# ScalarE makes the negative half of the first attention's features, one set of moments serves two norms, three projections go together, and the last loop's rows are fetched sooner

## What is computed

```python
h = tok(x, W); h = concat([cls, h])
h = h + attn0(layernorm(h))                # elu(q)+1, elu(k)+1, KV = sum K V over the images, @ Wo.T + bo
h = h + ffn0(layernorm(h))                 # see below
h = h + attn1(layernorm(h))                # causal linear attention, 16 heads
h = h + ffn1(layernorm(h))                 # shared SwiGLU + top-1 of 32 routed SwiGLU experts

def attn0(x):  Q = elu(x @ Wq.T + bq) + 1; K = elu(x @ Wk.T + bk) + 1; V = x @ Wv.T + bv; ...
def ffn0(x):
    xn = (x - mean(x)) * rsqrt(var(x) + 1e-5) * ln_scale + ln_bias
    x_attn = xn @ attn_w.T + attn_b + x
    eo = gelu(x_attn @ w1[e] + b1[e]) @ w2[e] + b2[e]      # expert e is fixed by the position
    return gelu(eo @ next_w.T + next_b)
def layernorm(x): return (x - mean(x)) / sqrt(var(x) + 1e-5)
```

## Time and profile before

| what | us |
|---|---|
| three runs of the kernel | 339.25, 343.43, 345.67 (median 343.43) |
| the profiled execution, its own time | 341.32 |
| its span, first to last instruction | 339.5 |
| tokens, 0 to 34.3 | 34.3, PE busy 24.4 |
| first attention, 34.3 to 65.3 | 31.0, PE busy 27.8 |
| start of ffn0, 65.3 to 88.8 | 23.5, PE busy 16.3 |
| rest of ffn0, 88.8 to 177.7 | 88.9, PE busy 86.5 |
| second attention and routing, 177.7 to 247.5 | 69.8, PE busy 62.6 |
| shared expert and first routed turns, 247.5 to 282.2 | 34.7, PE busy 33.1 |
| further turns, 282.2 to 316.9 | 34.7, PE busy 32.8, DMA share 0.90 |
| last turns and the loop, 316.9 to 339.5 | 22.6, PE busy 15.7 |

### The profile page before, as it was taken

How to read it: one execution, slowest core, us unless ns; L and a number is a source line. 1 busy time by engine, 2 the same in 40 slices (tenths; PEclk the granted TensorE clock), 3 DMA queues, 4 the chain that set the end, 5 groups by cost and what they waited for, 6 DMA issues and landing times.

```text
span 339.5 us, 6676 instructions
## 1 busy us (share of the span) xinstructions
PE 299.2 (88%) x2487; PEld 214.7 (63%) x2487; DVE 206.7 (61%) x595; ACT 138.0 (41%) x312; POOL 52.3 (15%) x72
## 2 busy tenths in 40 slices
PE   1997979758989999999999988989799899997965
PEld 1775547648889999999898666765355334552331
DVE  0355494323546557556557899865964899636726
ACT  1012231522332332323264666527334986515641
POOL 0111000011011001011000001010542001111842
PEclk9999797958999999999999999799999999997979
DMA  7999995000633724000000000399955838999541
GB/s 289 392 443 423 419 302 149 2 0 1 247 102 149 248 52 197 2 0 2 2 1 3 2 2 2 109 431 422 429 205 163 356 113 318 342 386 386 82 65 16
DMA packets 12762, 61.57 MB, mean 181 GB/s; under 512 B 1546, under 2 KB 7514, under 8 KB 9146
## 3 DMA queue, kind: packets, MB, share of 16 engines
q1 hardware_dynamic: 10746, 58.25, 45.1%
q0 software_dynamic: 1984, 2.89, 4.3%
HBM read 55.09 MB, written 6.04 MB: 180 GB/s over the span
## 4 chain that ended last, share of the span: by engine, by line
PE 64%; DVE 15%; DMA 12%; issue 4%; ACT 2%; POOL 1%; SPq 0%; DVEq 0%; ACTq 0%; POOLq 0%
PE P L359 16%; DMA arena<-experts_dram 10%; PE P L467 9%; PE P L479 9%; PE P L669 5%; PE P L611 4%; PE P L393 4%; PE P L523 4%; PE P L682 3%; PE P L455 2%; PE P L554 2%; DMA arena<-patches_dram 2%; DVE arena L1046 1%; DVE st L967 1%; DVE arena L1138 1%
## 5 line engine op out<-in xcount | busy, mean ns | idle before, releaser
L359 PE MATMUL P<-arena 128*104 128x256 f32 x288 | 73.8, 397 | 9.1 <-DMA arena<-patches_dram 6.9
L359 PEld LDWEIGHTS P<-arena 128*104 128x104 f32 x288 | 47.5, 177 | 22.3 <-issue 8.1
L1382 POOL TENSOR_TENSOR rstd<-var,mhalf 104x1 f32<-104x1 f32 x40 | 22.0, 550 | 206.1 <-DVE var L969 206.1
L669 PE MATMUL P<-arena,cols 128*32 128x512 f32 x288 | 34.7, 621 | 4.1 <-ACT cols L901 2.8
L876 ACT ACTIVATE arena<-arena 128x1024 f32 x31 | 31.6, 1051 | 14.2 <-SPq L338 8.6
L479 PE MATMUL P<-arena 128*128 128x104 f32 x256 | 29.9, 275 | 2.4 <-ACT arena L804 2.4
L479 PEld LDWEIGHTS P<-arena 128*128 128x128 f32 x256 | 29.7, 192 | 3.1 <-issue 1.4
L467 PEld LDWEIGHTS P<-arena 128*128 128x128 f32 x256 | 30.8, 197 | 1.3 <-issue 0.7
L467 PE MATMUL P<-arena 128*128 128x104 f32 x256 | 30.6, 279 | 0.5 <-issue 0.5
L804 ACT ACTIVATE arena<-P,arena 128x104 f32<-128x104 f32 x64 | 17.0, 348 | 28.7 <-PE P L467 28.7
L611 PE MATMUL P<-cols,arena 128*128 128x416 f32 x64 | 23.8, 520 | 1.8 <-DVE arena L1199 1.8
(11 more groups left out here) (209 smaller groups left out, 485.9 us busy)
## 6 DMA issues: line engine op xcount, KB each, us to landing
arena<-experts_dram SPq DMA_DIRECT2D x18, 1536.0 KB, 9.4
...
arena<-w_dram SPq DMA_DIRECT2D x1, 1024.0 KB, 10.2
...
```

What stands on the lines that cost most here:

```text
L359: last = mm(P[b][0:a.shape[1], col:col + D], a, rhs(c), start=(c == 0), stop=(c == chunks - 1))
L669: last = mm(P[b][part, :], xT[:, c, part], weights(u)[:, c * INNER:(c + 1) * INNER], start=(c == 0), stop=(c == DC - 1), tile_position=(0, ...
L1382: nc.gpsimd.tensor_tensor(rstd[:, :], var[:, :], mhalf[:, :], ALU.pow).then_inc(s["rstd_ready"], 1)
```

## The change

The edits make four pieces.

1. Features. ACT now reads the bank first: `Relu(-(x + b))` into `eA` (the negated bias is made once on DVE in `own`), then `Exp(-eA)`. DVE waits for ACT's read (`z0_sum`), makes max(x + b, 0) into `zA` in one instruction, and adds `eA`. The value tile 0 is read by DVE (`v0_evac(0)`) ahead of the last feature's addition.
2. Norms. `h1_norms` makes one set of moments of `h`. A second column of `var` holds var * (1 + eps) + eps^2; `power` works on both columns, and both normalised rows come from `h`. bo is added to all of `h` beforehand by one POOL instruction over 104 x 2048, behind the eighth norm; so DVE adds the projection straight into `h`.
3. Projections. `wo(0)`, `wo(1)` and `wo(2)` go to banks 0, 7 and 6 and stand ahead of the ffn0 steps; only wo(3) and later stay in them. `wo_read` is gone; `h0_ready` counts in its place.
4. The nop that gives `l_aim_ready` its first count stands in the first fixed turn, behind `aim_static()`.

```diff
+            for g in range(3):
+                wo(g)
             pe.wait_ge(s["wx_in"], 16)
...
-            lagged(GROUPS + 3, [(tr1, 1), (tr2, 3), (nx, 2), (xa, 1), (wo, 0), (up, 1), (but_last(qk1), 3), (but_last(v1), 3), (down, 1)])
+            lagged(GROUPS + 3, [(tr1, 1), (tr2, 3), (nx, 2), (xa, 1), (later_wo, 0), (up, 1), (but_last(qk1), 3), (but_last(v1), 3), (down, 1)])
...
             for n in range(8):
-                act.wait_ge(s["z0_ready"], n + 1)
-                A(eA[:, n % 2, :], eA[:, n % 2, :], ACT.Exp).then_inc(s["exp0_done"], 1)
+                w, m = n // 4, (n // 2) % 2
+                act.wait_ge(s["qk0_done"], n + 1)
+                if n >= 2:
+                    act.wait_ge(s["qk0_ready"], n - 1)
+                A(eA[:, n % 2, :], bank(n % 4, HALF), ACT.Relu, scale=-1.0, bias=own[:, 2 * w + m:2 * w + m + 1]).then_inc(s["z0_sum"], 1)
+                act.wait_ge(s["z0_sum"], n + 1)
+                A(eA[:, n % 2, :], eA[:, n % 2, :], ACT.Exp, scale=-1.0).then_inc(s["exp0_done"], 1)
...
+            V.tensor_scalar(own[:, 0:4], bcol_s[:, BQ0:BQ0 + 4], -1.0, None, ALU.mult).then_inc(s["zeroed"], 1)
...
-                    dve.wait_ge(s["qk0_done"], n + 1)
-                    if n >= 2:
-                        dve.wait_ge(s["qk0_ready"], n - 1)
-                    V.tensor_scalar(zA[:, n % 2, :], bank(n % 4, HALF), bcol_s[:, b:b + 1], None, ALU.add).then_inc(s["z0_sum"], 1)
                     dve.wait_ge(s["z0_sum"], n + 1)
-                    V.tensor_scalar_min(eA[:, n % 2, :], zA[:, n % 2, :], 0.0).then_inc(s["z0_ready"], 1)
+                    V.tensor_scalar(zA[:, n % 2, :], bank(n % 4, HALF), bcol_s[:, b:b + 1], 0.0, ALU.add, ALU.max).then_inc(s["z0_ready"], 1)
                 if n == 0:
                     continue
                 n -= 1
...
+                if n == 7:
+                    dve.wait_ge(s["brow_in"], 32)
+                    v0_evac(0)
                 dve.wait_ge(s["exp0_done"], n + 1)
-                V.scalar_tensor_tensor((qT, kT)[w][:, m, half * HALF:(half + 1) * HALF], zA[:, n % 2, :], 0.0, eA[:, n % 2, :],
-                                       ALU.max, ALU.add).then_inc(s["qk0_ready"], 1)
+                dve.wait_ge(s["z0_ready"], n + 1)
+                V.tensor_tensor((qT, kT)[w][:, m, half * HALF:(half + 1) * HALF], zA[:, n % 2, :], eA[:, n % 2, :], ALU.add)\
+                    .then_inc(s["qk0_ready"], 1)
...
             def h1_norms(g):
                 dve.wait_ge(s["wo_done"], g + 1)
-                V.tensor_tensor(xr2[:, g % 2, :], P[0][0:GT, 0:D], brow_s[0:GT, BO0, :], ALU.add).then_inc(s["wo_read"], 1)
-                dve.wait_ge(s["wo_read"], g + 1)
-                V.tensor_tensor(h[:, g, :], h[:, g, :], xr2[:, g % 2, :], ALU.add).then_inc(s["h0_ready"], 1)
+                if g == 0:
+                    dve.wait_ge(s["bo0_added"], 1)
+                V.tensor_tensor(h[:, g, :], h[:, g, :], P[wo_bank(g)][0:GT, 0:D], ALU.add).then_inc(s["h0_ready"], 1)
                 dve.wait_ge(s["h0_ready"], GROUPS + g + 1)
-                norm(h[:, g, :], xr[:, g % 2, :], "n_ready")
-                dve.wait_ge(s["n_ready"], GROUPS + 2 * g + 1)
-                norm(xr[:, g % 2, :], xr2[:, g % 2, :], "n_ready")
+                link(V.bn_stats(st[:, :], h[:, g, :]))
+                link(V.bn_aggr(mv[:, :], st[:, :]))
+                V.tensor_scalar(var[:, 1:2], mv[:, 1:2], 1.0 + EPS, EPS * EPS, ALU.mult, ALU.add)
+                V.tensor_scalar_add(var[:, 0:1], mv[:, 1:2], EPS).then_inc(s["var_ready"], 1)
+                norms[0] += 1
+                dve.wait_ge(s["rstd_ready"], norms[0])
+                V.tensor_scalar(xr2[:, g % 2, :], h[:, g, :], mv[:, 0:1], rstd[:, 1:2], ALU.subtract, ALU.mult).then_inc(s["n_ready"], 1)
+                V.tensor_scalar(xr[:, g % 2, :], h[:, g, :], mv[:, 0:1], rstd[:, 0:1], ALU.subtract, ALU.mult).then_inc(s["n_ready"], 1)
...
                 if q == 0:
                     aim_static()
+                    nc.vector.nop().then_inc(s["l_aim_ready"], 1)
...
-            nc.vector.nop().then_inc(s["l_aim_ready"], 1)
             nc.vector.nop().then_inc(s["l_y_ready"], 1)
...
+            pool.wait_ge(s["brow_in"], 32)
+            pool.wait_ge(s["n_ready"], GROUPS)
+            nc.gpsimd.tensor_tensor(h[:, :, :], h[:, :, :], brow_s[0:GT, BO0, :].unsqueeze(1).to_broadcast([GT, GROUPS, D]), ALU.add)\
+                .then_inc(s["bo0_added"], 1)
```

43 lines of the change are left out of this document (25 added, 18 removed).

## The result

The changed kernel took **338.28 us** (median of 4 runs, 335.89 to 338.78); the kernel before, timed beside it, 342.5. The ratio is 0.986 with a 95% interval of 0.981 to 0.991. The change gains 4.2 us. That is inside the range, and the interval lies clear of 1; but the forecast had 7.35, and the gain, 1.2 to 1.4%, is under the 2% beyond which the forecast counted a kernel as faster. The profiled execution took 338.18, of which 336.3 are the span (before: 341.32 and 339.5).

A forecast was written before the change was run, and what follows sets the result against it. PE bounds the kernel (64% of the span), so only places where it stands still count; -0.3 + 4.25 + 3.4 = 7.35 us off the median of 343.43 gives 336.1 us, range 332.6 to 340.2.

The forecast's parts named there:

- the ring: Features: relu, max and addition wait for one another, period 1.78 us (1.70 to 1.90), third value tile 0.3 later.
- wo(2): Second ffn0 step: this projection no longer stands between xa(1) and up(1), 0.35 us gained (0.3 to 0.45).
- a rival at 0.12: Features: relu costs 0.65 us or each hand-over shows, period 1.9, 0.75 us more lost, total 336.9; chance 0.12.
- bo on POOL: Behind the eighth norm: POOL's one addition over all of h is hidden, cost 0.
- The rival: Features: POOL's add holds up DVE, costing time beyond 6.8 us, slower than before from 14.2 us; chance 0.03.
- `power` on two columns at no cost: Norms on POOL: one column costs 0.55 us, nearly all start-up; the second column adds 0.
- Parts 2 and 3, the norm: Start of ffn0: one addition and the second norm go, net 1.98 us gained, tr1(0) at 69.3.
- wo(1)'s 1.1: First ffn0 step: without this projection between xa(0) and up(0), another 1.1 us gained.
- Case (b): Start of ffn0: clock falls in short stretches, rises after about 3 us, 3.9 us gained; the forecast, chance 0.45.
- case (c): Start of ffn0: clock low until after 78, 1.7 to 2.2 us gained; chance 0.20, shared with low loop clock.
- case (a): Start of ffn0: clock never falls, 5.4 us gained there, total 334.6; chance 0.20.
- Part 4: Last loop: rows arrive before PE asks, down product at full clock; 3.4 us gained, 1.9 if the clock falls.

The follow-up runs named there:

- add_first: Changed kernel with DVE's addition of the previous piece put ahead of max; 333.43 us, ratio 0.969 to the kernel before.
- features_only: Kernel before with only the new features (relu on ACT, new value tile order); 343.89 us, ratio 1.0067.
- both: Changed kernel with DVE's addition ahead of max, and `power` on one column wherever one is wanted; 333.03 us, ratio 0.988 to the kernel before.
- pool_late: Changed kernel with POOL's addition of bo held back until the second max is done; one execution, 341.94 us.
- ffn_only: Kernel before with only one set of moments, bo on POOL and three projections ahead; 338.62 us, ratio 0.988.
- projections_only: Kernel before with only wo(1) and wo(2) moved ahead of the ffn0 steps, norms as they were; one execution, 344.04 us.
- filler: Changed kernel with 10 matmul instructions nobody reads added at the start of ffn0; 339.31 us, ratio 0.990 to the kernel before.
- after_again: Changed kernel run again unchanged for a second profile; 338.78 us, ratio 0.992 to the kernel before.
- the first group: Experiments with one part at a time and the changed kernel again, on one chip; the kernel before took 342.53 us, median of 25 executions.

## Why the prediction came out as it did

By the profiled executions the gain is 341.32 - 338.18 = 3.1, where 7.35 was forecast. The missing 4.2 are, in order of size: wo(0) to down(0) 2.05 (1.4 of it the clock in up(0), 0.6 the links ahead of it), the ring 0.7, the end 0.5, wo(2) 0.25, `power` 0.15, and 0.55 of stretches that scatter. The predicted median, 336.1, missed by less (2.2), because this profiled execution of the change lies at the median of its runs and that of before lay 2.1 under the median on record then. That the median came so near is in part luck: place by place the change gave less than half of the sum.

- **Part 1, the ring: right mechanism, wrong size.** Right: one period is relu + max + addition, and the exponential is hidden. The failed step is "Relu reads a bank of 416 columns: ACT took 0.515 us for that shape". That row has no bias column, and is another function. With the bias column relu takes 0.607, and together with hand-overs the period is 1.885; six periods of 0.105 more are 0.63. No run has relu without the column, but a pair of rows of before would have warned: Identity on 104 columns from PSUM takes 349 ns with a bias column (L795) and 434 with a second column, for the scale (L789), so 85 ns more for one column, where relu is 92 over its row. 1.9 had been the upper bound and a rival at 0.12; it is what happened. The deeper miss is that, having drawn the ring, I priced it and did not ask whether the order on DVE could be other; `add_first` shows over 5 us in that.

The Trainium skill, "ScalarE: Activation LUTs", Rules for kernel authors, would have made relu 0.65, an estimate; the runs have 0.607, between the row taken and the page. Its advice to keep relu on VectorE holds for the change's order (`features_only` is 1.4 us longer), and not for the other order (`both` is 5.6 us under `old_features`).

- **bo on POOL: right.** 4.5 us, done at 39.32, before the first addition of two stored operands at 41.75. The rival needed over 6.8. But `pool_late` shows that the exclusion itself is real, and `ffn_only` that a minimum of one stored operand can suffer too.

The Trainium skill, "SBUF — State Buffer", Who interferes with whom, says this of the two-operand addition; `pool_late` agrees, 3.53 us for 0.58. "GPSIMD Engine Reference", section 3.1, says 4.5 us for the add; the run has 4.507.

- **`power` on two columns at no cost: wrong by a quarter.** "nearly all of it start-up" is true of 550 ns, but a second column adds 140 ns on 104 rows. It lies on the path of each norm that PE waits for: 0.14 at the start and 0.14 in ffn0.

- **Parts 2 and 3, the norm: right, 1.75 for 1.98** (tr1(0) behind wo(0)'s start: 5.94 to 4.19, in three profiles). Of the missing 0.23, 0.14 are `power`. wo(1)'s 1.1 was nearly right too (0.93 in `projections_only`), and up(0) starts 3.96 sooner than before, where the old pace had given 3.1.

- **The clock at ffn0: the term that was mis-sized.** (The old spell ended at 78.4, by the 0.61 of the earlier trace rows, not at 78.2.) Case (b) took the slow spell to fall on the transposes and xa(0), be short, and be over before up(0). The opposite happened: they ran at full clock and won 1.3, and the spell came in up(0), which is continuous work: 6.68 in the first profile, 5.42 in the second, for 3.79 at full clock. Against before, 1.85 and 3.1 were gained. "rises again after about 3 us" holds for one of them and not for the other: it was low from 74.4 to 81.3, 6.8 us, in the first profile and for 3.4 us in the second. So the first profile's size is that of case (c), the second's lies between the cases, and neither has their course. The profiles with this code and no filler all fall into these two kinds: of the eight, up(0) took 5.4 in five (low for 3.4 us) and 6.7 to 6.9 in three (low for 6.8 us). And the full-clock place that the cases start from was set 0.6 too high: `filler` has 4.8 for the 5.4 of case (a), since the transposes came 0.23 later than forecast and up(0) began another 0.3 later behind them.

- **wo(2): 0.11 for 0.35.** The row behind it, 89.49 for up(1)'s start, could not tell 0.3 from its own gap of issue.

- **Part 4: 2.9 for 3.4.** SP, PE and clock came as forecast: the fetch at 315.75 (317.5 forecast), no wait for a DMA, L1301 4.35 behind the transposes (3.8 forecast). ACT's copy began 1.52 behind the transposes' start (1.22 in the earlier trace rows), and PE 0.24 behind its end, not 0.07; these two make the 0.5. What the prediction didn't see is what is late next: POOL's queue of indirect additions of 1.55 to 2.1 us each, which in `after_again` took 2.1 us of this.

- **What no step had.** The clock in a stretch 140 us behind the edits moves with them, by 0.8 in the change's favour, and by 0.9 to 2.4 against the filler. Why is **open**. The clock stays up there in all nine profiles of kernels that have their projections ahead and no filler, and falls in the five others; but that is a pattern, and no run was made for it. The clock also makes much of the scatter of the times: of the 25 executions of the kernel before in the first group, the shortest, 337.05, had a mean granted clock of 0.978, and the longest, 346.81, one of 0.959.
